# A gated graph layer: U is made one block later inside the edge sums, W and V become one product, and the split of W into three parts moves over three engines and five buffers

## The reference, cut to what matters

```
Wh = x @ W_w + W_b
Uh = x @ U_w + U_b
Vh = x @ V_w + V_b
out_src = Wh * attn_l
out_dst = Wh * attn_r
sigma = sigmoid(out_src[src] + out_dst[dst])
h = Uh + segment_sum(Vh[src] * sigma, dst) / (segment_sum(sigma, dst) + 1e-06)
h = layernorm(h) * gamma + beta
x = x + relu(h)
```

## Time and profile before

| what | us |
|---|---|
| median of three runs | 3003.66 (3002.97 to 3009.3) |
| the profiled execution | 3003.86 |
| its span, first to last instruction | 3002.2 |
| `stage_gated_in`, first gather to the last store's issue | 1639.3 to 1733.8 |
| `stage_strips`, gathers | 1738.4 to 2758.4 |
| mean granted TensorE clock, share of full speed | 0.908 |

### The profile page before, as it was taken

The page is one execution under the profiler, slowest core; times in us unless marked ns, Lnnn a source line. Parts: engine busy times, 40 slices in busy tenths (PEclk is TensorE's granted clock), DMA queues, the critical chain, the costliest instruction groups (busy, mean ns, idle before and its releaser), DMA issues. The chain is left out here.

```text
span 3002.2 us, 50772 instructions
## 1 busy us (share of the span) xinstructions
PE 2495.9 (83%) x17111; PEld 1245.4 (41%) x17164; DVE 2350.3 (78%) x5375; ACT 1158.3 (39%) x2327; POOL 1364.5 (45%) x1627
## 2 busy tenths in 40 slices
PE   5999979999969999966997947677676777767598
PEld 3666655333355333344665512233332333323365
DVE  6888889999959999977444847777777777777477
ACT  5777720000020000012222435666666666566421
POOL 2999920000000000001830867777777777775055
PEclk8999989999989999976998977888888888888799
DMA  4000000000020000031432687888888888888343
GB/s 125 12 11 12 10 36 15 15 15 15 5 82 15 15 15 15 5 100 45 121 96 64 203 249 238 250 259 256 259 255 252 257 257 260 255 252 250 121 150 107
DMA packets 210756, 373.53 MB, mean 124 GB/s; under 512 B 52554, under 2 KB 140559, under 8 KB 208682
## 3 DMA queue, kind: packets, MB, share of 16 engines
q0 software_dynamic: 75536, 238.14, 26.4%
q1 hardware_dynamic: 131737, 128.66, 13.5%
q10 hardware_dynamic: 3200, 3.21, 0.4%
HBM read 324.84 MB, written 50.04 MB: 125 GB/s over the span
## 5 line engine op out<-in xcount | busy, mean ns | idle before, releaser
L1167 PE MATMUL dense_p_o<-dense_W,feat 128*32 128x512 f32 x7200 | 789.8, 595 | 17.5 <-DVE dense_W L1099 17.5
L1099 DVE SCALAR_TENSOR_TENSOR dense_W<-layer_B,steep,cnt 128x512 f32<-128x512 f32 x1200 | 796.7, 750 | 3.3 <-DVE dense_W L1099 2.0
L2466 POOL DMA_INDIRECT Wd<-tab_d,ixq x544 | 519.4, 955 | 171.1 <-issue 166.2
L1167 PEld LDWEIGHTS dense_p_o<-dense_W,feat 128*32 128x32 f32 x7200 | 281.9, 110 | 494.5 <-issue 390.3
L1577 POOL MEMSET edst<- 128x782 int32 x1 | 0.8, 750 | 921.9 <-POOLq L1216 921.9
L2644 PE MATMUL strips_p_sg<-strips_sv,strips_oh 128*32 128x512 f32 x2000 | 313.6, 704 | 101.0 <-DVE strips_sv L2509 101.0
L2632 PE MATMUL strips_p_b<-strips_wrs,strips_ohT 96*128 96x256 bf16 x1000 | 177.8, 308 | 208.8 <-DVE strips_ohT L2480 190.6
L732 POOL TENSOR_SCALAR mix_L<-mix_back,encode_lowT 128x128 bf16<-128x128 f32 x520 | 328.6, 650 | 18.7 <-PE mix_p_c L891 18.6
L2573 ACT ACTIVATE strips_p_s<-strips_tv 128x1024 f32<-128x1024 f32 (+1 forms) x250 | 225.2, 901 | 157.3 <-DVE strips_sv L2509 144.5
L1123 ACT COPY dense_part<-dense_p_o 128x512 f32<-128x512 f32 x36 | 18.8, 596 | 639.7 <-PE dense_p_o L1167 639.7
L2466 POOL DMA_INDIRECT strips_G<-tab_d,ixq x240 | 228.9, 954 | 73.1 <-issue 72.8
(11 more groups left out here) (543 smaller groups left out, 3899.3 us busy)
## 6 DMA issues: line engine op xcount, KB each, us to landing
strips_row<-dlr_d SPq DMA_DIRECT2D x250, 96.0 KB
ew<-in_ew SPq DMA_DIRECT2D x16, 1024.0 KB, 5.4
layer_B<-rise_d SPq DMA_DIRECT2D x12, 1024.0 KB, 4.6
hx_d<-hrow SPq DMA_DIRECT2D x24, 512.0 KB, 2.7
Wd<-tab_d,ixq POOLq DMA_INDIRECT x544
Wd<-in_fWd SPq DMA_DIRECT2D x8, 1024.0 KB, 9.2
tab_d<-feat SPq DMA_DIRECT2D x50, 130.0 KB, 1.9
tab_d<-gated_in_rowg SPq DMA_DIRECT2D x25, 256.0 KB, 2.0
```

The lines of the kernel that those rows point to most:

```text
L1099: o = nc.vector.scalar_tensor_tensor(out=out, in0=rise, scalar=C.steep[:, q * H + h:q * H + h + 1], in1=count, op0=ALU.max, op1=ALU.mult)
L1167: m = nc.tensor.matmul(p_o[c % 2][h * MT:(h + 1) * MT, a, 0:n], feat[:, q, h, lo:lo + MT], W[t % 3][:, h, 0:n], start=(q == 0), stop=(q == ...
L2466: gp.indirect_dma_start(out=G[n % RING][:, j, :], out_offset=None, in_=C.tab3[:, :], in_offset=bass.IndirectOffsetOnAxis(ap=index, axis=0) ...
```

## The change

**In `stage_gated_in`** U is no longer made. `w3` holds W and V, and both are one product of 512 columns with two products for the bias. `xT` is stored to a new DRAM table `xT_d` in place of U. `row`, `xT` and the PSUM tiles `p_a` have four buffers where they had two, and `wf` and `wp` have five where they had three. The split is shared out: ACT rounds `wf` to the first part (`first_part`), POOL subtracts (`rest`), ACT rounds to the second part (`second_part`), POOL subtracts again (`third_part`, one turn later than `rest`). DVE's third multiplication is gone.

**In `stage_strips`** SP loads the transposed rows `xTu` in place of U, one block ahead, and the U weights once. `project(b)` makes U of block b in 256 columns of `p_h`. It stands in the first step of block b+1, between `expand` and `sums`; for the last block it opens the final tail. DVE adds U straight from `p_h`. PE gets three new waits that keep `p_h` free, SP a wait on `project`, and the idle products read `b3S` times zero weights. `stage_gate`, the path not taken, gets a loop that makes U for itself.

```diff
 stage_gated_in
-        w3 = sb("w3", [P, KC, 3 * D])
+        w3 = sb("w3", [P, KC, 2 * D])
 POOL
-                for b in range(NB + late):
+                for b in range(NB + late + 1):
                     if b < NB:
                         gather(b)
-                    if b >= late:
-                        split(b - late)
+                    if late <= b < NB + late:
+                        rest(b - late)
+                    if b >= late + 1:
+                        third_part(b - late - 1)
+                def third_part(b):
+                    k = b % NW
+                    gp.wait_ge(s_w1, b + 1)
+                    nc.gpsimd.tensor_tensor(wp[k][:, 2, :], wf[k][:, :], wp[k][:, 1, :], ALU.subtract).then_inc(s_sp, 1)
 DVE
-                    nc.vector.tensor_tensor(wp[m][:, 0, :], p_a[k][:, 0, 0:D], ar[:, :], ALU.mult).then_inc(s_row, 1)
 ACT
-                    nc.scalar.copy(us[k][:, :], p_a[k][:, 1, 0:D]).then_inc(s_pass, 1)
+                def second_part(b):
+                    act.wait_ge(s_sub, b + 1)
+                    nc.scalar.copy(wp[b % NW][:, 1, :], wf[b % NW][:, :]).then_inc(s_w1, 1)
...
-                    if b >= 1:
-                        taken(b - 1, (b - 1) % 2)
+                    if 2 <= b <= NB + 1:
+                        taken(b - 2, (b - 2) % 4)
+                    if 2 <= b <= NB + 1:
+                        first_part(b - 2)
+                    if b >= 4:
+                        second_part(b - 4)
 PE
-                    for a, lo, w in ((0, 0, D), (1, D, 2 * D)):
-                        for kc in range(KC):
-                            nc.tensor.matmul(p_a[k][:, a, 0:w], xT[k][:, kc * P:kc * P + P], w3[:, kc, lo:lo + w], start=(kc == 0), stop=False)
+                    for kc in range(KC):
+                        nc.tensor.matmul(to, xT[b % 4][:, kc * P:kc * P + P], w3[:, kc, :], start=(kc == 0), stop=False)
 stage_strips
 SP
-                        if i == 0 and b >= 1 and b + 1 < NB:
-                            sp.wait_ge(s_ur, b)
+                        if i == 8 and 0 <= b and b + 1 < NB:
                             load_u(b + 1)
 PE
+                    def project(b):
+                        if b == 0:
+                            pe.wait_ge(s_wu, 16)
+                            pe.wait_ge(s_ones, 1)
+                        else:
+                            pe.wait_ge(s_ur, b)
+                        if b >= 2:
+                            pe.wait_ge(s_he, FC * (b - 1))
+                        pe.wait_ge(s_u, 16 * (b + 1))
+                        for kc in range(KC):
+                            nc.tensor.matmul(p_h[:, F - D:F], xTu[:, kc * P:kc * P + P], wu[:, kc, :], start=(kc == 0), stop=False)
+                        nc.tensor.matmul(p_h[:, F - D:F], ones[:, :], C.b3S[:, D:2 * D], start=False, stop=True).then_inc(s_up, 1)
...
+                        if g % QC == 0 and g > 0:
+                            project(g // QC - 1)
```

More of the change, by code:

```diff
@@ L2138, in parts @@
                 def parts(b):
[L2139 to L2142 removed]
+                    sp.wait_ge(s_sp, b + 1)
+                    sp.dma_start(C.wr_d[:, b * P:(b + 1) * P, :].rearrange("s p d -> p s d"), wp[b % NW][:, :, :]).then_inc(s_wd[b % NW], 16)
+                for b in range(NB + 4):
                     if b < NB:
[L2144 to L2146 removed]
@@ L2147, in _ @@
-                for k in range(3):
-                    sp.wait_ge(s_wd[k], 16 * ((NB + 2 - k) // 3))
+                        turned(b)
+                    if 1 <= b <= NB:
+                        back(b - 1, (b - 1) % 4)
+                    if b >= 4:
+                        parts(b - 4)
+                for k in range(NW):
+                    sp.wait_ge(s_wd[k], 16 * ((NB + NW - 1 - k) // NW))
+                for k in range(4):
+                    sp.wait_ge(s_xTd[k], 16 * ((NB + 3 - k) // 4))
@@ L2225, in _ @@
                     if b >= 3:
-                        back(b - 3, (b - 3) % 2)
+                        back(b - 3, (b - 3) % 4)
                 v.wait_ge(s_x, NB)
@@ L2263, in _ @@
                 normal(0, 0)
-                for b in range(NB + 1):
+                for b in range(NB + 4):
                     if b + 2 < NB:
@@ L2319, in stage_strips @@
         G = [C.Wd[:, k * FC * D:(k + 1) * FC * D].rearrange("p (h d) -> p h d", h=H) for k in range(NE)] + [sb(f"G{k}", [P, H, 2 * D]) for k in range(NE, RING)]
-        row = [sb(f"row{k}", [ST, H, P], BF16) for k in range(RR)]; ipt = sb("ipt", [ST, P]); ip = sb("ip", [ST, 1])
-        oh = [sb(f"oh{k}", [P, H, QP]) for k in range(4)]; nil = sb("nil", [P, 2 * D], BF16)
+        row = [sb(f"row{k}", [ST, H, P], BF16) for k in range(RR)]; ip = sb("ip", [ST, 1]); ones = sb("ones", [ST, P], BF16)
+        oh = [sb(f"oh{k}", [P, H, QP]) for k in range(4)]; nil = sb("nil", [ST, P], BF16); wu = sb("wu", [P, KC, D])
         ohT = [sb(f"ohT{k}", [ST, H * P], BF16) for k in range(2)]
@@ L2940, in load_u @@
                         sp.dma_start(U[b % 4][:, :], C.u_d[b * P:b * P + P, :]).then_inc(s_u[b % 4], 16)
+                    sp.dma_start(wu[:, :, :], A["w3"][:, D:2 * D].rearrange("(c p) f -> p c f", p=P)).then_inc(s_wu, 16)
+                    for b in range(NB + 1):
+                        if b < NB:
+                            if b >= 2:
+                                sp.wait_ge(s_up, b - 1)
+                            sp.dma_start(U[b % 2][:, :], C.xT_d[b * P:b * P + P, :]).then_inc(s_ux[b % 2], 16)
+                        if b >= 1:
+                            sp.wait_ge(s_uc, b)
+                            sp.dma_start(C.u_d[(b - 1) * P:b * P, :], U[2 + (b - 1) % 2][:, :]).then_inc(s_us[(b - 1) % 2], 16)
+                    sp.wait_ge(s_us[0], 16 * ((NB + 1) // 2))
+                    sp.wait_ge(s_us[1], 16 * (NB // 2))
                     for b in range(4):
@@ L3042, in _ @@
                 with when_even(C, act, 0):
+                    for b in range(NB):
+                        act.wait_ge(s_up, b + 1)
+                        if b >= 2:
+                            act.wait_ge(s_us[b % 2], 16 * (b // 2))
+                        nc.scalar.copy(U[2 + b % 2][:, :], (p_l, p_r)[b % 2][:, 0:D]).then_inc(s_uc, 1)
                     def root(c):
@@ L3080, in _ @@
                 with when_even(C, pe, 0):
+                    pe.wait_ge(s_wu, 16)
+                    pe.wait_ge(s_ones, 1)
+                    for b in range(NB):
+                        pe.wait_ge(s_ux[b % 2], 16 * (b // 2 + 1))
+                        if b >= 2:
+                            pe.wait_ge(s_uc, b - 1)
+                        to = (p_l, p_r)[b % 2][:, 0:D]
+                        for kc in range(KC):
+                            nc.tensor.matmul(to, U[b % 2][:, kc * P:kc * P + P], wu[:, kc, :], start=(kc == 0), stop=False)
+                        nc.tensor.matmul(to, ones[:, :], C.b3S[:, D:2 * D], start=False, stop=True).then_inc(s_up, 1)
+                    pe.wait_ge(s_uc, NB)
                     pe.wait_ge(s_wd, 64)
@@ L3390, in build @@
     C.rise_d = dram("rise_d", (NB * H, P))
-    C.u_d = dram("u_d", (NP, D))
+    C.u_d = dram("u_d", (NP, D)); C.xT_d = dram("xT_d", (NP, KC * P))
     C.wr_d = dram("wr_d", (3, NP, D), BF16)
@@ L3451, in build @@
             stage_gated_in(nc, C, A)
-            bias.close()
             C.Wd = ctx.enter_context(nc.sbuf_tensor("Wd", [P, NE * FC * D], F32, side="right"))
```

148 lines of the change are left out of this document (81 added, 67 removed).

## The result

The changed kernel took **3015.99 us** (median of 9 runs, 3013.82 to 3019.11), the kernel before beside it 3006.53 (9 runs, 3000.77 to 3009.3). The ratio is **1.0029, 95% interval 1.0021 to 1.0037**: slower by 0.2 to 0.4%. The forecast was 3011, with a range from 2996 to 3022. The profiled execution took 3019.11 us, its span 3017.4. One execution of the kernel before, beside the third group of experiments, took 8227 us and is left out of all medians and ratios given here.

A forecast was written before the change was run, and what follows sets the result against it. The prediction took PE, with DVE close behind, to pace stage_gated_in, and POOL's gathers to bound stage_strips. Its terms, +8.2 + 0 - 1.2 + 0 = +7 us on the profiled 3003.86, gave 3011, range 2996 to 3022.

The forecast's parts named there:

- What bounds: PE paces stage_gated_in, DVE close behind; POOL's gathers bound stage_strips; time changed in stage_gated_in shifts what follows one for one.
- The circle: stage_gated_in, blocks 8 to 24: waits through DVE, ACT, POOL and the gather take 7.5 us per two blocks, +8.2 us.
- The hold-up by POOL: stage_gated_in: POOL's subtraction can delay DVE's small `off` operation, up to +3.6 us over eight pairs; taken as 0.
- The pairs: stage_gated_in from block 8: block starts alternate 2.5 and 5.0 us apart, DVE waiting some 2.4 us for `yb` every second block.
- The tail of the stage: stage_gated_in, block 24's start to the last store: 14.4 us becomes about 13.2, -1.2 us.
- The first eight blocks: stage_gated_in: the first `back` comes some 1.5 us later, and the next blocks earn it back; 0, within 1.
- The strips: stage_strips: `project` fits in PE's idle time before the sums, gathers still take 999 us; 0.
- The circle doesn't bind: Rival, stage_gated_in: DVE's 2.55 us a block sets the pace, -11.4 and -1.2 us, giving 2991; chance 0.19.
- The clock: Rival, stage_gated_in: pauses drop PE to half clock, 4.4 us a block, +12 to +18 us, 3016 to 3022; chance 0.12.
- a product of over 2 us in mid-stage: Sign, stage_gated_in: a 512-column product taking over 2 us in mid-stage would show the prediction wrong.
- The strips' steps: Rival, stage_strips: block steps become the bound, +17 us on top of +7, giving 3028; chance 0.07.
- given back: Rival, stage_strips: `project` keeps PE awake and the 5 us lag of the steps could go, giving 3006; chance 0.10.

The follow-up runs named there:

- broken on ACT and on POOL: Two edits to the changed kernel: second_part at the head of ACT's turn, 3000.9 us; third_part two turns later on POOL with seven buffers, 3001.39 us.
- lengthened by a known amount: Changed kernel with one extra ACT copy of 1024 columns before second_part in each block: 3032.95 us, ratio 1.0084.
- the half alone: Kernel before with only stage_strips changed; its stage_gated_in stores the transposed rows in place of U: 3007.62 us, ratio 1.0005.
- the first broken circle: Changed kernel with ACT's second_part moved from the end of its turn to the head: 3000.9 us, ratio 0.9979.
- its first half alone: Changed stage_gated_in with the strips of before, which load transposed rows where U stood, U left out of the computation: 3021.09 us, ratio 1.005.

## Why the prediction was right, point by point

**What bounds.** Right in what the sum uses: that the stage's length shifts all that follows one for one shows in the table, +8.2 in `stage_gated_in`, then +0.7 over the strips' gathers. Half wrong in who sets the pace of the stage before. In that trace PE counts as busy for all of the time both where blocks come 3.13 us apart (blocks 8 to 12) and where they come 3.31 apart (15 to 22), with the same products, so its full share doesn't show that it is the bound. From block 15 to block 22 the offset took 0.61 us in each, beside POOL's subtraction, and DVE waited for nobody:

```profile
1691.43 0.61 DVE L2196 SCALAR_TENSOR_TENSOR gated_in_off<-gated_in_mv,gated_in_rstd 128x1 f32<-128x1 f32 x1
...
1693.29 0.47 DVE L2184 SCALAR_TENSOR_TENSOR X<-gated_in_yb,kept,X 128x256 f32<-128x256 f32 x1
```

DVE's turn of 2.85 and 0.45 of hold-up are 3.30, and the next addition comes 3.31 after that of 1689.98. In these eight blocks DVE, held up by POOL, set the pace. The forecast didn't suffer, since the circle then bound above either of them.

**The circle.** Right in mechanism, in direction and in place. It was to bind from block 8 on: the first eight blocks took 22.34 us for 22.72, and DVE's next wait for `yb` after block 0's comes at block 8. It was broken on ACT and on POOL with the same result, and lengthened by a known amount with the reckoned one. Its size was 7.5 us; measured are 7.82 on the mean, so the term was +10.5 in place of +8.2. The steps of the pair shown above against the prediction's: addition to `xn` 1.92 (1.64), `xn` to `xT` 0.50 (0.51), to the first part 0.52 (0.54), the two parts 0.72 (0.72), hand-over 0.07, third part to gather 0.82 (0.82), gather to the next addition 3.33 (3.2 and a hand-over). Only the first is clearly off, by 0.28. Over all eight pairs the middle steps stay within 0.01 us of these; the first lies between 1.65 and 2.04 (mean 1.90), the last between 2.96 and 3.66 (mean 3.30).

**The hold-up by POOL, taken as 0 with up to 3.6 kept.** This is the term that was mis-sized, and the 0.28 is its price. What it was put at 0 for, fewer meetings of the two engines, held only for `off`. It didn't fall on `off`, which took 0.16 to 0.17 in all 16 blocks, but on the first addition of a pair: 0.82, 0.84, 0.87, 0.75, 0.50, 0.82, 0.48 and 0.75 us for the eight pairs from block 8, where the second ones take 0.47 or 0.48. That is 0.25 on the mean, 8 x 0.25 = 2.0 of the 2.3 us that the circle's term was short of, and the circle's first step follows it: 1.65 and 1.67 us in the two pairs whose addition took 0.48 and 0.50, 1.92 to 2.04 in the six others. The price was inside the bound, the instruction was another. That POOL makes these additions long is read from where they end (last section), not tested.

**The pairs.** Expected 2.5 and 5.0 us apart, measured 2.9 and 4.8 (additions at 1684.30, 1687.22, 1692.06, 1694.86, 1699.94). The sum is right, its parts are less far apart. DVE's second wait, for PE's product in 7 of these 16 blocks (8.7 us), comes within the slack of a pair. Its wait for `yb` was 11.1 us over seven blocks, 1.6 each, where some 2.4 were expected.

**The tail of the stage** -1.2, measured -1.2. **The first eight blocks** 0, measured -0.4. **The strips** 0: measured +0.7 in one execution, and 1.0005 for the half alone. POOL's 24 blocks of gathers (first gather of block 0, 1749.71, to that of block 24, 2749.39) took 999.7 us for 999.

```profile
2749.39 0.94 POOL L2493 DMA_INDIRECT Wd<-tab_d,ixq  x1 [0.30 <-issue]
```

**The sum.** +7 forecast and 3011. The medians stand 9.5 us apart, of which the stage has 8.2 by the profiles. The rest, +0.7, +1.7 and +1.6 behind the stage, is of the size by which unchanged stretches differ from run to run (the last stretch of the table lay between 184.6 and 189.4 us over the kernels of this study); it was only read, not tested. Of the 5 us between the forecast of 3011 and the median of 3016, 2.9 are the kernel before, which stood at 3006.53 over nine executions and at 3003.66 over the three that the forecast started from. The profiled execution, 15 us above that of before, overstates the change by the 3.1 us of the first line and its like.

**The rivals.** *The circle doesn't bind*: refuted by every wait above. It promised too much as well: 12 to 13 us below the kernel before, where with the circle broken the kernel lies 6 to 11 us below it; its pace of 2.55 became 2.86 by the hold-up and the second circle. *The clock*: it did fall, to 0.86 on the mean, with a product of 3.08 us after a pause of 2.64 us, as that rival had it (the products slowed down behind four of the five pauses of over 2.6 us; behind one of 2.63 they took 1.97). The prediction had named a product of over 2 us in mid-stage as a sign of being wrong; six of these 16 took 2.08 to 3.65. The sign was badly chosen: the middle steps of the circle are the same to 0.01 us in the pairs with slow and with fast products, and the additions of blocks 10 and 20, the only two that follow slow products without a noted wait for `yb`, still start 0.23 and 0.14 us later than DVE's multiplication ahead of them allows (0.56 and 0.47 behind its start, where 0.33 is usual). So the low clock set nothing here that these rows show. Nor did it start by itself: with the circle broken and no product taken away it is back at full speed by itself (window of blocks 8 to 24 of the first broken circle):

```profile
1665.90:1712.40 46.50, 39.33 (x131) 17.17 (x129) 43.72 (x145) 31.03 (x97) 36.66 (x48) 1.00 0.79 245
```

So the low clock followed from the circle's pauses. The Trainium skill (TensorE: Matmul & The Clock Gate, "Why this matters for your kernels") warns of pauses between bursts of products; the trace agrees as to the fall, and shows that here it had no price. *The strips' steps* and *given back*: neither is seen; three times the work of `project` moved nothing.

## What to carry to other kernels

When work moves to another engine, follow the queue of the engine that now waits: a prefetch that stands behind such a wait is no prefetch any more, and its whole latency joins the loop. Here two casts of 0.7 us together, on an engine with half its time free, closed a loop that cost 10 us, and one line moved within a turn, or a step made two turns later with two more buffers, made the changed kernel 0.5 to 0.6% faster. When no engine is full and the stage got longer, add the loop up from one turn of the timeline; and price a step by how often it lies on the loop (here once in two blocks), not by how often it is run.

## What the runs showed of the hardware

- VectorE and GpSimd hold each other up by whole instructions, in both directions. A 128x1 operation of 0.16 us took 0.41, 0.61 or 0.62 us and ended within 0.03 us of the end of GpSimd's subtraction; the subtraction took 0.85 to 0.91 us in place of 0.67 where VectorE's addition had started first. This is what the Trainium skill states (SBUF — State Buffer, "SBUF: two separate sides": a lock, held for the whole instruction, that an operation of VectorE with two inputs in SBUF takes against one of GpSimd that reads SBUF), and the rows agree. `reciprocal` and the addition of a constant, with one input, kept 0.15 us beside the same subtractions.
- Moving the held-up instruction didn't free it here: who waits went by which engine had started first, and that order shifted with the move (0.41 became 0.62).
- Not understood: the long first additions of a pair. Seven of the eight ended 1.29 to 1.34 us after the start of a gather on GpSimd, the five long ones among them having begun 0.42 to 0.56 us after it, and GpSimd's next subtraction took 0.83 to 0.89. (The eighth, 0.82 us long, had begun 0.15 us after a subtraction and ended 0.29 after its end.) It comes back in three more kernels with the circle, the changed one run again, its first half alone and the one with `project` three times: from block 8 on, 13 additions that began 0.33 to 0.52 us after a gather's start took 0.78 to 0.98 us and ended 1.30 or 1.31 after it. The gather itself takes 0.97, so it looks as if they waited for its end. But in the kernel before, the same addition began 0.4 us after a gather's start as well, with a subtraction right behind that gather too, and took 0.48. What makes the difference wasn't tried.
